# Interleaving the butterflies of one W2 tile with the transposes of the tile before it

## The reference

```python
xn = layernorm(x)                                    # x: 8 x 2048 x 2048
s = attention(xn, Wq, Wk, Wv, Wg, ...)               # 16 heads, window 1024, gated, rms-normed
hidden = silu(xn @ W1.T) * (xn @ W3.T)               # W1, W3: 8192 x 2048
hidden = fwht(hidden)                                # Walsh-Hadamard over the 8192, / sqrt(8192)
g = silu(hidden @ W2.T)                              # W2: 2048 x 8192
out = x + s * g
```

## Time and profile before

| | us |
|---|---|
| median of two runs | 6703.43 (6632.6 and 6774.26) |
| profiled execution | 6298.45 |
| its span, slowest core | 6296.9 |
| TensorE (matmul) busy | 4497.6 (71%) |
| VectorE busy | 1877.7 (30%) |
| ScalarE busy | 1475.6 (23%) |
| GpSimd busy | 411.9 (7%) |
| hidden stage, about | 2230 to 4773 |
| final stage, about | 4830 to 6297 |

### The profile page before, as it was taken

How to read it: one execution, slowest core, us unless ns; L and a number is a source line. 1 busy time by engine, 2 the same in 40 slices (tenths; PEclk the granted TensorE clock), 3 DMA queues, 4 the chain that set the end, 5 groups by cost and what they waited for, 6 DMA issues and landing times.

```text
span 6296.9 us, 68795 instructions; the slowest of 8 cores (6269.6 to 6296.9 us)
## 1 busy us (share of the span) xinstructions
PE 4497.6 (71%) x23424; PEld 2148.4 (34%) x23424; DVE 1877.7 (30%) x3024; ACT 1475.6 (23%) x3690; POOL 411.9 (7%) x692
## 2 busy tenths in 40 slices
PE   2876566656756678888877888888894765838567
PEld 1333323423423433434433343334442322313223
DVE  6434444543542533333233333333310000000000
ACT  2324424424433432222222222222220000000000
POOL 1000000010000001111111111111110000000000
PEclk9985586576576589999998999999997988969889
DMA  5110110020010023333333333333324344343532
GB/s 142 14 14 8 20 14 7 7 28 7 7 19 16 8 58 68 67 67 72 71 75 68 67 68 67 67 68 67 67 57 145 105 151 140 120 161 129 178 107 107
DMA packets 163568, 429.36 MB, mean 68 GB/s; under 512 B 50208, under 2 KB 103584, under 8 KB 138656
## 3 DMA queue, kind: packets, MB, share of 16 engines
q0 software_dynamic: 68352, 197.18, 15.4%
q1 hardware_dynamic: 92576, 211.00, 10.0%
q10 hardware_dynamic: 2304, 16.78, 0.7%
HBM read 445.86 MB, written 92.27 MB: 85 GB/s over the span
## 4 chain that ended last, share of the span: by engine, by line
PE 48%; DMA 17%; DVE 15%; ACT 10%; issue 8%; POOL 1%; DVEq 0%; ACTq 0%; SPq 0%; POOLq 0%
PE PBIG L1054 14%; PE PBIG L971 12%; PE PBIG L957 11%; PE PBIG L522 5%; ACT p_bf L707 4%; DVE ST L702 4%; DMA w2pp<-w2st 4%; DMA sTb<-s_scr 3%; DMA hidc<-hid_scr 2%; PE PBIG L727 2%; DVE pT_bf L750 2%; DMA w2c<-w2pp 2%; DMA w2x<-w 2%; DMA w2y<-w 1%; ACT sqs L533 1%
## 5 line engine op out<-in xcount | busy, mean ns | idle before, releaser
L1054 PE MATMUL PBIG<-hidc,w2c 128*128 128x512 bf16 x4096 | 956.8, 388 | 252.6 <-DMA hidc<-hid_scr 225.7
L971 PE MATMUL PBIG<-xnT,w3T 128*128 128x512 bf16 x4096 | 959.8, 389 | 214.2 <-DVE hidb L978 214.2
L957 PE MATMUL PBIG<-xnT,w1T 128*128 128x512 bf16 x4096 | 949.0, 386 | 0.0
L1054 PEld LDWEIGHTS PBIG<-hidc,w2c 128*128 128x128 bf16 x4096 | 391.2, 99 | 791.1 <-issue 385.6
L522 PE MATMUL PBIG<-wq_bf,xnT 128*128 128x512 bf16 x2304 | 574.1, 412 | 111.9 <-DMA wq_bf<-wq 75.8
L971 PEld LDWEIGHTS PBIG<-xnT,w3T 128*128 128x128 bf16 x4096 | 397.6, 100 | 666.4 <-issue 262.1
L957 PEld LDWEIGHTS PBIG<-xnT,w1T 128*128 128x128 bf16 x4096 | 400.8, 99 | 457.5 <-issue 32.3
L978 DVE TENSOR_TENSOR hidb<-sg_scr,PBIG 128x512 bf16<-128x512 f32 x256 | 175.5, 686 | 1229.0 <-PE PBIG L924 815.4
L763 PE MATMUL PBIG<-v_st,pT_bf 128*128 128x128 bf16 x1728 | 274.9, 296 | 291.4 <-ACT pT_bf L744 204.6
L1069 DVE TENSOR_TENSOR wbf<-gfb,sTb 128x512 bf16<-128x512 f32 x64 | 44.3, 692 | 1364.1 <-ACT gfb L1063 883.0
L963 ACT ACTIVATE sg_scr<-PBIG 128x512 f32<-128x512 f32 x256 | 152.9, 597 | 1000.7 <-PE PBIG L957 722.4
(11 more groups left out here) (95 smaller groups left out, 3864.0 us busy)
## 6 DMA issues: line engine op xcount, KB each, us to landing
w2c<-w2pp SPq DMA_DIRECT2D x128, 1024.0 KB, 4.8
w1nat<-w POOLq DMA_DIRECT2D x64, 512.0 KB, 5.7
w3nat<-w POOLq DMA_DIRECT2D x64, 512.0 KB, 7.8
hid_scr<-hidb POOLq DMA_DIRECT2D x256, 128.0 KB, 2.0
w2pp<-w2st POOLq DMA_DIRECT2D x64, 512.0 KB, 4.8
hidc<-hid_scr SPq DMA_DIRECT2D x32, 1024.0 KB, 8.0
xt<-x SPq DMA_DIRECT2D x16, 1024.0 KB, 5.9
w2x<-w POOLq DMA_DIRECT2D x8, 2048.0 KB, 14.9
```

The lines of the kernel that those rows point to most:

```text
L957: e.matmul(o, l, r, start=s, stop=st, skip_group_check=True) for i in range(ND)]
L971: e.matmul(o, l, r, start=s, stop=st, skip_group_check=True) for i in range(ND)]
L1054: e.matmul(o, l, r, start=s, stop=st, skip_group_check=True)
```

## The change

The function that appends a tile now splits it in two: the load with the twelve butterfly halves, and the 16 batches. The batches are held back until the next tile is appended, and then go into the list in turns with the load and the butterfly halves of that next tile. The first tile's load and butterflies go in alone. The batches of the last tile are appended behind the loop over aa.

```diff
-        def emit_w2pre_load_and_bfly(dt):
+        def build_w2pre_parts(dt):
...
-            w2all.append(lambda dt=dt, src=src, skey=skey: em.dma(
+            loadside = [lambda dt=dt, src=src, skey=skey: em.dma(
                 "gpsimd", f"sw2_{dt % 2}", src.ap()[:, :],
-                w2_in[128 * dt:128 * (dt + 1), :], writes=(skey,)))
+                w2_in[128 * dt:128 * (dt + 1), :], writes=(skey,))]
...
-            for bt in range(16):
-                w2all.append(lambda dt=dt, bt=bt, src=src, skey=skey:
-                             emit_one_w2batch(dt, bt, src, skey))
+            batches = [lambda dt=dt, bt=bt, src=src, skey=skey:
+                       emit_one_w2batch(dt, bt, src, skey)
+                       for bt in range(16)]
+            return loadside, batches
+
+        def emit_w2pre_load_and_bfly(dt):
+            loadside, batches = build_w2pre_parts(dt)
+            prev = w2pre_pending_batches[0]
+            w2pre_pending_batches[0] = batches
+            if prev is None:
+                w2all.extend(loadside)
+                return
+            n = max(len(prev), len(loadside))
+            for j in range(n):
+                if j < len(prev):
+                    w2all.append(prev[j])
+                if j < len(loadside):
+                    w2all.append(loadside[j])
+
+        w2pre_pending_batches = [None]
...
+        if w2pre_pending_batches[0] is not None:
+            w2all.extend(w2pre_pending_batches[0])
+            w2pre_pending_batches[0] = None
         while w2all:
             w2all.pop(0)()
```

More of the change, by code:

```diff
@@ L864, in emit_w2pre_load_and_bfly @@
                                               two=2, b=blk)
[L865 to L874, removed]
@@ L875, in emit_w2pre_load_and_bfly @@
-            for bt in range(16):
-                w2all.append(lambda dt=dt, bt=bt, src=src, skey=skey:
-                             emit_one_w2batch(dt, bt, src, skey))
+                loadside.append(lambda frv=frv, tov=tov, frk=frk, tok=tok:
+                                em.op("vector", lambda e, o=tov[:, :, 0, :],
+                                      a_=frv[:, :, 0, :], b_=frv[:, :, 1, :]:
+                                      e.tensor_add(o, a_, b_),
+                                      reads=(frk,), writes=(tok,)))
@@ new lines, in build_w2pre_parts @@
+                loadside.append(lambda frv=frv, tov=tov, frk=frk, tok=tok:
+                                em.op("vector", lambda e, o=tov[:, :, 1, :],
+                                      a_=frv[:, :, 0, :], b_=frv[:, :, 1, :]:
+                                      e.tensor_sub(o, a_, b_),
+                                      reads=(frk,), writes=(tok,)))
+            batches = [lambda dt=dt, bt=bt, src=src, skey=skey:
+                       emit_one_w2batch(dt, bt, src, skey)
+                       for bt in range(16)]
```

## The result

| | before | after |
|---|---|---|
| all runs, median (lowest to highest) | 6540.64 (6290.23 to 6822.43), 26 runs | 6468.41 (6339.33 to 6847.18), 27 runs |
| ratio after to before, 95% interval | | 1.0057 [1.0039, 1.0076] |
| profiled execution | 6298.45 | 6349.34 |
| its span, slowest core | 6296.9 | 6347.8 |

The change makes the kernel about half a per cent slower. The sharpest number is the span of the slowest core of such a group: its median is 6298 us for cores 0 to 3 and 6294 for cores 4 to 7 before (12 and 14 spans), and 6345 and 6344 after (23 and 19 spans), so +48 us. The two profiled executions differ by 50.9.

A forecast was written before the change was run, and what follows sets the result against it. TensorE was taken to set the hidden stage's pace, stopped by late W2 loads. Tile changes +47 (332 against 285), interleaving 0 and tail +24 gave +71 us, put on the median 6703.4: 6774 us, range 6340 to 6850.

The forecast's parts named there:

- What bounds it: Hidden stage: TensorE sets the pace, stopping 214.2 us at the W3 product behind VectorE, which waits for late W2 loads.
- (1): Load to first butterfly: one batch now stands between, load still behind four stores on GpSimd; gains at most one iteration.
- (2): VectorE's copy of a tile's first batch into w2st waits for all four stores, 22.1 us; TensorE stops at shared bank pb6.
- (3): Price of the new waits at 14 tile changes, in two kinds: 332 us against 285 removed, +47 us.
- kind A: Tile change with batch 15 first in its pair, next batch 0 second: stops of 21.6 and 6.9 us, together 32.6.
- kind B: Tile change with batch 15 second in its pair: one stop of 12.7 us, 14.8 with the slow group.
- the price of the old change: Tile changes in the kernel before: 20.3 us by period, 18.7 by pieces; taken as 19, x 15 = 285 us removable.
- (4): Single batches interleaved with load and butterflies in the loop: cost 0, at most 48 us if cover went.
- (5): Last tile's 16 batches and four stores run after the loop: +24 us, with 3 for the lower clock.
- (b): Rival, faster: the stop at pb6 does not bite, TensorE's two banks cover the copy's wait; -229, 6474 us; chance 0.06.
- (c): Rival: stores faster in the new place, 3.2 us each; -68, 6635 us; chance 0.07.
- (d): Rival, slower: the chain of stores stretches to cadence 6.5, load to 18.7 us; +155, 6858 us; chance 0.13.

The follow-up runs named there:

- sp_before: The kernel before, with the four chained w2pp stores of a tile issued on SP instead of GpSimd: spans 6063 and 6075 us, -227 against before.
- sp_after: The changed kernel, with the four chained w2pp stores of a tile issued on SP instead of GpSimd: spans 6344 (one) and 6342 us, -2 against after.
- w2st_keys: The changed kernel with one w2st key per batch, each store waiting only for its own quarter's batches: spans 6230 and 6226 us, -117 against after.
- w2_banks: The changed kernel with the W2 transposes in banks pb4 and pb5 in turn instead of pb6: spans 6225 and 6222 us, -121 against after.

## Why the prediction was right or wrong, point by point

**What bounds it, and (1): right.** The load stood behind the chained stores; sp_before shows it directly. In the changed kernel the load's waits are 102 us, inside the 80 to 120 that the text named.

**(2), the new wait: right.** It came at the instruction, 14 times, with the bank that was named, and sp_after, w2st_keys and w2_banks each show one link of it: the stores, the key, the bank. The single waits were 13.9 to 24.9 us, where 15 to 21 were named.

**(3), the price of a change: right in its kinds, a little high in its sizes.** The stops of kind A were 19.8 to 20.9 us where I had 21.6 (the copy was free at 21.4 and not 22.1, and TensorE's group ended a microsecond later), the second ones 4.2 to 8.1 with a mean of 5.9 where I had 6.9, those of kind B 11.8 to 13.4 where I had 12.7. All 21 together are 272.8 us against 288. By the period, from the copy at 2506.82 to the one at 4313.41 twelve tiles on, a tile takes 150.5 us, which less 126.8 is 23.7 for a change; 14 of them are 332, the figure of the sum. That the two agree is luck. The 21 stops together were put 16 us too long. The groups at the lower clock behind them were put too short (about 2 us each, where they cost some 2.5), and a few small pieces were not counted; together these make up the same 16 us.

**The step that failed is the price of the old change**: "I take 19, x 15 changes = 285 us that the change could remove". By the period it was 20.3, and so 305; the text had this number and took one near the 18.7 of its pieces. The pieces leave out 1.6 us a change, in part the slow group behind the flushed Hadamard matmul in every second one (5.00 us for 3.62); the rest I have not placed. Since the new side came out at its full 332, the 20 us missing on the old side went straight into the difference: 332 - 305 = +27 where the sum had 332 - 285 = +47. Less the 20.2 of the batches that leave the loop, the loop is +7, and the trace has +5.1. The sum had +27 for it.

**(4), interleaving itself costs 0: right.** A single batch takes the 1.26 us of one in a pair, here from 2513.22 to 2514.48 in the changed kernel:

```profile
2513.22 0.39 PE L923 MATMUL PBIG<-IDENT,w2y 128*128 128x128 bf16 x4
...
2514.48 3.61 PE L974 MATMUL PBIG<-xnT,w1T 128*128 128x512 bf16 x16
```

**(5), the tail: right.** 44.7 and 3 for the lower clock were expected from the last group to SP's first load, 49.0 were measured. The batches with their last copy took 26.8 us, where 24.6 were expected (most of them 1.60 us each, as from 4802.53 to 4804.13, since they ran at the lower clock). The first store came 1.3 us later, and the chain took 20.9 us to SP's load and not 22.1.

**The sum.** +71 was forecast, and +48 to +51 measured in spans. In the terms of the sum, the exchange of waits is +27 (forecast +47), and the tail, less the 20.2 us of work that it took over from the loop, +25 (forecast +24). So the change is slower by two pieces of about the same size: the tile changes became dearer (14 of 23.7 us for 15 of 20.3), and the last tile's batches and stores stand where nothing covers them.

**The level: wrong.** "I put the +71 on the median shown: 6774" took the median of two executions for the level of the kernel. Over 26 executions the median before is 6540.64, and after it is 6468.41, which is 306 us under the forecast. The profiled execution was the one to add to: 6298.45 + 71 is 6370, 0.3% from the profiled execution after. The range 6340 to 6850 held the measured median only because it was made wide enough for nearly everything.

**The rivals.** (b) and (c) are refuted: w2_banks removes the bank and TensorE still stops, and the stores kept their cadence, 5.3 to 5.8 us between issues at the first change, with TensorE and VectorE standing still. (d) did not come: the longest single wait of the chain was 6.0 us, and 6.2 before.

**The Trainium skill's figure for a store.** By "DMA: Bandwidth & Descriptors" in the Trainium skill, section "Anatomy of one DMA — SWDGE (gpsimd) path", one store would be an estimate of 3.2 us and the chain 12.8. Here a store took 4.8 us to land in the median and 5.3 to 5.8 from one issue to the next, and even with the waits between them taken out the four were done only after 13.3 to 13.9 us. The measurement decides. The traces have no store with larger pieces, so they do not tell whether the pieces of 256 B are the reason.

## What to carry to other kernels

When an order is interleaved to spread an engine's load, ask of every buffer in the moved work who last read it and how long ago: here a copy moved from six iterations behind four stores to directly behind them, and took over the wait that was to be hidden. Where a load is late, look first at what stands before it in the list of its issuing engine; moving that one item ahead of the work it can overlap was worth 216 us, and the interleaving, which moved 29 items a tile, lost 48. Before you book work as removed from a loop, see where it runs instead. And when a small difference is the sum of two large ones, measure both sides in the same way, by the period of a repeating unit if there is one.

## What the hardware showed that I had not expected

Four stores of 512 KB in flight together finish in about two thirds of the time of the same four one behind the other (13.3 to 13.9 us against 21.4), though each of them takes nearly twice as long (8.6 against 4.8 us).

A store of the same kind issued on SP is not dearer than on GpSimd in the median: landing took 3.8 us in sp_after and 4.5 in sp_before, against 4.8. But the longest wait of one chained store for the one before was 19.6 us in sp_after and 23.0 in sp_before, against 6.0 in the changed kernel and 6.2 in the one before, where the stores are on GpSimd and the 2 MB load of W2 stands behind them. At the change of sp_after that is told above, the load was in flight beside the slow stores; the other long waits I did not look at one by one.

TensorE went to the lower of its two clocks in the tail and stayed there: from 4785 to 4808 us the granted clock was 0.50, though it was busy 13.7 of the 23 us, with two short pieces of work in each 1.6 us. Four transposes took 0.59 us there, where the first ones behind the loop still took 0.38.
